# ScalarE evicts V and applies the later first normalizations; V's bias goes through the output weights

## The chip, the cores and the metric

One core of one Trainium2 chip runs the kernel. The metric is device time in microseconds (us) of one execution. Engines are named as in the profile: PE is TensorE, DVE is VectorE, ACT is ScalarE, POOL is GpSimd, SP is SyncE, which issues every DMA. A measurement of this kind tells a difference of about one per cent from none.

## What is computed

16 sequences of 128 tokens with 512 features pass through three residual blocks in 32-bit floats:

```python
x = x + attn(layernorm(x))      # 16 heads of 32, ALiBi bias, 30*tanh(s/30), causal softmax, Wo, bo
x = x + xattn(layernorm(x))     # 128 context tokens per sequence, masked softmax, readout
x = x + ffn(layernorm(x))       # gate/up/down with weights rounded to fp8 e4m3, width 1536
```

In the first block `v = h @ Wv.T + bv` and `out = (probs @ v) @ Wo.T + bo`, and each row of `probs` sums to one.

## The kernel before

The sequences are worked on in G = 4 groups of GT = 4 (512 tokens). For each group g four stages hg = 0 to 3 run, one for each four heads. One stage on PE is: `scores(g, hg)` into PSUM banks 2 to 5 (S_BANK, one for each head); the Q and K projections of the next stage into banks 0 and 1 (Q_BANK, K_BANK); other work of this stage; then `context(g, hg)`, which multiplies probabilities by V into bank 6 (C_BANK) and their sums into bank 7 (E_BANK). The other work is, at hg 0, the four V projections `v_proj` into banks 6, 7, 0, 1; at hg 1, the output projection `wo_proj` of the group before, into the same four banks; at hg 2, `turn_x`, the transposes of the next group's normalized input. Every full-precision product is made of three products of rounded halves (hi x hi, hi x lo, lo x hi), so that one projection of 128 columns is 12 matmuls of 128x512. The order on each engine is written out by hand, and each engine works strictly in it; semaphores tie them together. `take(item, b)` gives a bank to a new item once the item before it is drained, and `wait_drained` and `wait_filled` are its other two ends.

ACT, in each stage, takes tanh out of the four score banks, evicts Q with its bias (`q_out`), applies the exponential to four tiles, evicts K (`k_out`), rounds the context (`context_high`), and at hg 2 rounds the transposed input (`x_high`). POOL applies the causal mask to the four tiles (`causal`, L638), makes the low half of the context (`low_part`, L632), the reciprocal roots (`norm_scale`, L627), adds the output bias to the residual (`add_bo`, L659). DVE evicts V with its bias (`v_out`, L994), normalizes the context (`normalize_context`: reciprocal L1008, four shuffles, product L1017, after which C_BANK is free), makes the low half of the input (`x_low`, L988), adds the output projection to the residual (`wo_out`), takes statistics (`norm_stats`), and normalizes (`norm_apply`, L982).

The second block of group g - 2 lies in hg 3 and in hg 0 of later groups, in seven steps `cross(g, k)`: transpose, scores, softmax, transpose (bank 5), and the readout product into bank 3 (RO_BANK), which DVE adds to the residual with a weight (L1032, L1034, L1038).

Beside it, 36 slabs of feed-forward weights are rounded. DVE prepares a slab (`prepare_slabs`, L1058 and L1060; slab n waits until slab n - 2 is rounded), POOL rounds it (`round_slabs`, L645 and L647), ACT looks for overflows (`flag_slabs`, L811 and L813), and SP stores it and loads the sixth slab after it, once its place is flagged. Three tables, PREPARED, ROUNDED and FLAGGED, say for each group how many slabs fall in each of its four stages. After the last stage PE goes on to the feed-forward products (L262, L398), which run back to back to the end.

```python
if n > 1:
    dve.wait_ge(q_rounded, n - 1)
dve.tensor_scalar(m.bitcast(U32), w.bitcast(U32), EXPONENT_BITS, None, ALU.bitwise_and)
```

## Time and profile before

| what | us |
|---|---|
| median of three runs | 579.44 |
| lowest and highest of them | 578.35, 582.94 |
| the profiled execution | 580.64 |
| its span, first to last instruction | 578.9 |
| PE busy in the span | 551.5 |
| DVE, POOL, ACT busy | 339.7, 279.8, 243.2 |

The profile is of one execution, 1.74 us longer than its span. A timeline row gives the start in us from the span's start, the length, the engine, the line of the code, and in square brackets how long the engine stood idle before it and what released it. Rows merge instructions of one form. Ends of matmuls are modelled: the next one starts a little before the end that a row gives. The granted clock is a share of TensorE's full 2.4 GHz.

### The profile page before, as it was taken

The page shows a single profiled execution, that of the slowest core. Times are in us where ns is not written, and L with a number is a line of the kernel's source. Part 1 is how long each engine was busy: PE and PEld are TensorE (multiplying, and loading weights), DVE is VectorE, ACT ScalarE, POOL GpSimd, SP SyncE. Part 2 cuts the span into 40 slices and gives each one's busy share as a digit, 9 for nine tenths or more (in the row PEclk, how much of TensorE's full clock was granted, in tenths as well). Part 3 has the DMA queues.
Part 4 walks back from the last instruction along what each step waited for, and adds up shares of the span by engine and source line. Part 5 has one row for each costly group of instructions (what it writes and reads, how often), then busy time and mean ns, then how long its engine had stood idle before and what let it go on. Part 6 is the DMA issues. An engine that isn't in the chain of part 4 may idle for free.

```text
span 578.9 us, 9934 instructions
## 1 busy us (share of the span) xinstructions
PE 551.5 (95%) x3890; PEld 452.1 (78%) x3890; DVE 339.7 (59%) x674; ACT 243.2 (42%) x471; POOL 279.8 (48%) x284
## 2 busy tenths in 40 slices
PE   2998998999989999899999999999999999999997
PEld 2787876888768887687887787888888888888885
DVE  6478737975488754986767674345533564233322
ACT  3537882668626676237753242023311333023310
POOL 5756769855667666888767230023400343013310
PEclk9999999999999999899999999999999999999999
DMA  8861223441215420194181902100001000100001
GB/s 263 301 200 43 71 75 108 129 165 41 88 57 145 148 66 27 55 308 135 56 307 41 303 0 92 54 19 1 1 31 43 1 0 1 44 30 0 2 18 54
DMA packets 44189, 50.98 MB, mean 88 GB/s; under 512 B 3184, under 2 KB 25712, under 8 KB 44144
## 3 DMA queue, kind: packets, MB, share of 16 engines
q1 hardware_dynamic: 44144, 50.36, 26.9%
q8 instruction: 31, 0.51, 0.4%
q14 instruction: 14, 0.11, 0.1%
HBM read 36.72 MB, written 13.63 MB: 87 GB/s over the span
## 4 chain that ended last, share of the span: by engine, by line
PE 80%; POOL 7%; DVE 6%; ACT 4%; issue 1%; DMA 1%; SPq 0%; DVEq 0%; ACTq 0%
PE bank L262 52%; PE bank L398 15%; PE bank L257 3%; PE bank L336 2%; PE bank L318 2%; PE bank L354 2%; PE bank L343 2%; POOL probs L638 2%; DVE q_m L1058 1%; DVE q_m L1060 1%; POOL x_res L659 1%; PE bank L310 1%; POOL rstd L627 1%; POOL q_w L647 1%; POOL q_w L645 1%
## 5 line engine op out<-in xcount | busy, mean ns | idle before, releaser
L262 PE MATMUL bank<-reduced 128*128 128x512 f32 x1536 | 363.0, 395 | 1.6 <-DVE reduced L988 1.6
L262 PEld LDWEIGHTS bank<-reduced 128*128 128x128 f32 x1536 | 287.6, 189 | 64.4 <-issue 3.3
L742 POOL TENSOR_TENSOR f_parts<-fused,f_parts 128x512 fp32r<-128x512 f32 x48 | 62.2, 1295 | 174.8 <-ACT f_parts L929 174.8
L911 ACT ACTIVATE tanh_g<-bank,half_gate 128x512 f32<-128x512 f32 x48 | 33.1, 689 | 152.5 <-PE bank L262 152.3
L398 PE MATMUL bank<-reduced,f_parts 128*128 128x512 f32 x384 | 89.0, 391 | 0.0
L398 PEld LDWEIGHTS bank<-reduced,f_parts 128*128 128x128 f32 x384 | 71.8, 188 | 15.6 <-issue 0.8
L638 POOL TENSOR_SCALAR_AFFINE_SELECT probs<-probs 128x512 f32<-128x512 f32 x64 | 41.6, 681 | 61.8 <-ACT probs L794 61.8
L1174 DVE SCALAR_TENSOR_TENSOR silu<-tanh_g,bank 128x512 f32<-128x512 f32 x48 | 32.9, 686 | 57.4 <-ACT tanh_g L911 57.4
L789 ACT ACTIVATE probs<-bank 128x512 f32<-128x512 f32 x64 | 33.0, 602 | 50.1 <-PE bank L318 47.4
L645 POOL TENSOR_TENSOR q_w<-q_w,q_m 128x512 f32<-128x512 f32 x36 | 46.9, 1302 | 4.2 <-DVE q_m L1060 4.2
L647 POOL TENSOR_TENSOR q_w<-q_w,q_m 128x512 f32<-128x512 f32 x36 | 47.2, 1312 | 2.8
L1181 DVE SCALAR_TENSOR_TENSOR fused<-bank,fuse_c,silu 128x512 f32<-128x512 f32 x48 | 36.0, 751 | 17.6 <-PE bank L262 16.9
L1192 DVE TENSOR_TENSOR y_sb<-bank,down_c 128x512 f32<-128x512 f32 x16 | 11.1, 692 | 55.8 <-PE bank L398 55.8
L257 PE MATMUL bank<-identity,xn 128*128 128x128 f32 x192 | 26.8, 285 | 10.8 <-DVE xn L982 9.6
L794 ACT ACTIVATE probs<-probs 128x512 f32<-128x512 f32 x64 | 35.8, 625 | 0.0
L1058 DVE TENSOR_SCALAR q_m<-q_w 128x512 uint32<-128x512 uint32 x36 | 29.6, 822 | 7.7 <-POOL q_w L647 7.6
L1060 DVE TENSOR_SCALAR q_m<-q_m 128x512 f32<-128x512 f32 x36 | 33.0, 918 | 1.2
L929 ACT ACTIVATE f_parts<-fused 128x512 fp32r<-128x512 f32 x48 | 29.9, 623 | 8.6 <-DVE fused L1181 8.5
L971 DVE BATCH_NORM_STATS2 bn<-x_res 128x6 f32<-128x512 f32 x48 | 31.7, 685 | 2.8 <-DMA x_res<-in_x 2.2
L257 PEld LDWEIGHTS bank<-identity,xn 128*128 128x128 f32 x192 | 23.4, 148 | 12.5 <-issue 9.9
L811 ACT ACTIVATE q_j<-q_w 128x512 f32<-128x512 f32 x36 | 22.4, 622 | 24.2 <-POOL q_w L647 16.0
L336 PE MATMUL bank<-probs,sums_to 128*32 128x128 f32 x512 | 27.1, 283 | 5.2 <-POOL probs L638 3.0
(86 smaller groups left out, 536.2 us busy)
## 6 DMA issues: line engine op xcount, KB each, us to landing
quantized<-q_w SPq DMA_DIRECT2D x36, 256.0 KB, 3.3
reduced<-quantized SPq DMA_DIRECT2D x12, 512.0 KB, 7.5
memT_sb<-in_memT SPq DMA_DIRECT2D x16, 256.0 KB, 4.7
mem_sb<-in_mem SPq DMA_DIRECT2D x16, 256.0 KB, 5.5
out<-y_sb SPq DMA_DIRECT2D x16, 256.0 KB, 2.0
x_res<-in_x SPq DMA_DIRECT2D x3, 1024.0 KB, 7.0
q_w<-in_gate_w SPq DMA_DIRECT2D x12, 256.0 KB, 3.2
q_w<-in_up_w SPq DMA_DIRECT2D x12, 256.0 KB, 3.3
```

The costliest lines, as they stand in the source:

```text
L257: ins = pe.transpose(dst[:, k * S:(k + 1) * S], src[:, k * P:(k + 1) * P], identity[:])
L262: ins = pe.matmul(dst, stationary, moving, start=(n == 0), stop=(n == len(pairs) - 1))
L336: ins = pe.matmul(sums[rows, 0:S], sums_to[:, i, :], probs[:, j, i, :], start=(i == 0), stop=(i == GT - 1))
L398: ins = pe.matmul(dst[:], part[:, f, t], down_q[:, f], start=(f + n == 0), stop=(f + n == FT))
L638: pool.affine_select(out=probs[:, j], in_=probs[:, j], compare_op=ALU.is_ge, fill=0.0, base=0, pattern=[[0, GT], [1, S]], channel_multipli ...
L645: pool.tensor_tensor(w, w, m, ALU.add).then_inc(q_sum, 1)
L647: pool.tensor_tensor(w, w, m, ALU.subtract).then_inc(q_rounded, 1)
L742: pool.tensor_tensor(f_lo[:, f, :], fused[:, f % 2, :], f_hi[:, f, :].bitcast(F32), ALU.subtract).then_inc(f_lo_ready, 1)
L794: act.activation(probs[:, j], probs[:, j], ACT.Exp, scale=CAP).then_inc(exped, 1)
L1058: dve.tensor_scalar(m.bitcast(U32), w.bitcast(U32), EXPONENT_BITS, None, ALU.bitwise_and).then_inc(q_step, 1)
L1060: dve.tensor_scalar(m, m, MIN_NORMAL, ROUNDER, ALU.max, ALU.mult).then_inc(q_prepared, 1)
L1181: dve.scalar_tensor_tensor(fused[:, f % 2, :], ups[:], fuse_c[:, f:f + 1], silu2[:, f % 2, :], ALU.mult, ALU.mult).then_inc(drain_sem(("U" ...
```

## The change

- V is evicted by ACT without its bias (`v_out` moves from DVE to ACT, after `context_high` in stage 0, with the overflow look of slabs between).
- The bias of V is carried through the output weights instead: `bias_through` puts 12 matmuls of 128x512 between the second and third V projection of group 0, with the bias broadcast as stationary operand, into bank 5 (PT_BANK). DVE adds the result to `bo_b` (`bias_out`), and POOL's `add_bo` of group 0 waits for that and comes after the causal mask. The bias is loaded as 128x4 instead of broadcast as 128x512.
- Three later normalizations, those of groups 2 and 3 for their first block and that of group 0 for its feed-forward block (`norm_apply(g + 1)` for g = 1, 2, 3), are applied by ACT, with a shift that DVE makes (`norm_shift`, two instructions on 128x4). Group 1's stays on DVE.
- On ACT the four exponentials stand directly behind the four tanh in stages 1, 2 and 3, and `q_out` after them; at stage 2 `k_out` comes before `q_out` and `context_high` after both. Stage 0 keeps its order.
- The last readout of a group takes Q_BANK instead of RO_BANK, and the transposes at stage 2 take K_BANK before Q_BANK.
- In group 0 statistics of group 1 come before the slabs, POOL rounds no slab ahead of the causal mask in stages 2 and 3, and the three tables are changed.

The diff, without declarations and unchanged neighbours:

```diff
-ROUNDED = ((2, 1, 2, 1),) + ((4, 3, 0, 2),) * (G - 1)
-FLAGGED = ((0, 2, 1, 2),) + ((3, 4, 0, 2),) * (G - 1)
-PREPARED = ((3, 1, 2, 1),) + ((4, 3, 0, 2),) * (G - 1)
+ROUNDED = ((0, 2, 1, 2), (4, 4, 0, 2)) + ((4, 3, 0, 2),) * (G - 2)
+FLAGGED = ((0, 0, 1, 1), (4, 5, 0, 2)) + ((3, 5, 0, 2),) * (G - 2)
+PREPARED = ((2, 1, 1, 2), (4, 4, 0, 2)) + ((4, 3, 0, 2),) * (G - 2)
...
-            def cross(g, k):
+            def cross(g, k, readout=RO_BANK):
...
                     i = k - 3
-                    dst, done = take(("RO", g, i), RO_BANK)
+                    dst, done = take(("RO", g, i), readout)
...
+            def bias_through():
...
+                pe.wait_ge(bv_split, 2)
+                pe.wait_ge(w_lo_made, WO_PART + 1)
+                dst, done = take(("BO",), PT_BANK)
+                products(dst[:], [(part[:, k:k + 1].to_broadcast([P, P]), w[:, k]) for k in range(KT)
+                                  for part, w in ((bv_hi, wo_hi), (bv_hi, wo_lo), (bv_lo, wo_hi))]).then_inc(done, 1)
...
                     v_proj(g, i, (C_BANK, E_BANK, Q_BANK, K_BANK)[i])
+                    if g == 0 and i == 1:
+                        bias_through()
                     if g >= 2 and i != 2:
-                        cross(g - 2, (4, 5, None, 6)[i])
...
+                        cross(g - 2, (4, 5, None, 6)[i], RO_BANK if i < 3 else Q_BANK)
...
                 for i in range(GT):
-                    turn_x(g + 1, i, (S_BANK, S_BANK + 1, Q_BANK, K_BANK)[i])
+                    turn_x(g + 1, i, (S_BANK, S_BANK + 1, K_BANK, Q_BANK)[i])
...
             weights(V_PART)
-            for dst, src in ((bv_b[:], bv.partition_broadcast(P)), (bo_b[:], bo.partition_broadcast(P)),
+            for dst, src in ((bv_c[:], bv), (bo_b[:], bo.partition_broadcast(P)),
...
                 pool.wait_ge(xn_ready[0], (g + 1) * GT)
+                if g == 0:
+                    wait_drained(pool, ("BO",))
...
                 slabs = slabs_at(ROUNDED, g, 0)
-                if g == 0:
-                    for i in range(GT):
-                        add_bo(g, i)
-                else:
+                if g:
...
                 else:
+                    for i in range(GT):
+                        add_bo(g, i)
...
                 slabs = slabs_at(ROUNDED, g, 2)
-                round_slabs(slabs[:1])
+                if g:
+                    round_slabs(slabs[:1])
...
                 low_part(g, 1)
-                round_slabs(slabs[1:])
+                round_slabs(slabs[1:] if g else slabs)
...
                 slabs = slabs_at(ROUNDED, g, 3)
-                round_slabs(slabs[:1])
+                if g:
+                    round_slabs(slabs[:1])
...
                 low_part(g, 2)
-                round_slabs(slabs[1:])
+                round_slabs(slabs[1:] if g else slabs)
...
             ffn_low(0, 1)
-            flag_slabs(flagged[:1])
...
                 ffn_low(0, f)
-                flag_slabs(flagged[f - 1:f])
                 round_slabs(late[f - 1:f])
+                flag_slabs(flagged[f - 2:f - 1])
...
+            def v_out(g, i):
+                src = wait_filled(act, ("V", g, i))
+                act.activation(v[:, i, :], src[:], ACT.Copy).then_inc(drain_sem(("V", g, i)), 1)
...
+            def norm_apply(g):
+                act.wait_ge(shift_made, g - 1)
+                for i in range(GT):
+                    act.activation(xn1[:, i, :], token_tile(g % G, i), ACT.Identity, bias=shift[:, i:i + 1],
+                                   scale=rstd[0][:, i:i + 1]).then_inc(xn_ready[0], 1)
...
                     context_high(g - 1, 3)
-                for k in range(4, 7):
-                    flag_slabs(flagged[k - 4:k - 3])
-                    if g >= 2:
-                        cross(g - 2, k)
+                for i in range(GT):
+                    if i < 3:
+                        v_out(g, i)
+                        if g >= 2 and i < 2:
+                            cross(g - 2, 4 + i)
+                        flag_slabs(flagged[i:i + 1 if i < 2 else None])
+                    else:
+                        v_out(g, i)
...
                     tanh(g, 1, j)
-                q_out(g, 2)
...
                     exp(g, 1, j)
+                q_out(g, 2)
...
                     context_high(g, 0)
+                else:
+                    norm_apply(g + 1)
...
                     tanh(g, 2, j)
-                context_high(g, 1)
-                q_out(g, 3)
...
                 k_out(g, 3)
+                q_out(g, 3)
+                context_high(g, 1)
...
                         tanh(g, 3, j)
+                    for j in range(4):
+                        exp(g, 3, j)
                     q_out(g + 1, 0)
-                    exp(g, 3, 0)
-                    exp(g, 3, 1)
...
                         cross(g - 1, 0)
-                    exp(g, 3, 2)
-                    exp(g, 3, 3)
...
-            def v_out(g, i):
-                src = wait_filled(dve, ("V", g, i))
-                dve.tensor_tensor(v[:, i, :], src[:], bv_b[:], ALU.add).then_inc(drain_sem(("V", g, i)), 1)
+            def bias_out():
+                src = wait_filled(dve, ("BO",))
+                dve.tensor_tensor(bo_b[:], src[:], bo_b[:], ALU.add).then_inc(drain_sem(("BO",)), 1)
...
+            def norm_shift(g):
...
+                dve.wait_ge(rstd_ready[0], g + 1)
+                dve.tensor_scalar(shift[:], mv[0][:, :, 0], -1.0, None, ALU.mult).then_inc(shift_step, 1)
+                dve.wait_ge(shift_step, g - 1)
+                dve.tensor_tensor(shift[:], shift[:], rstd[0][:], ALU.mult).then_inc(shift_made, 1)
...
             dve.tensor_tensor(fuse_c[:], gate_c[:], up_c[:], ALU.mult).then_inc(fuse_c_made, 1)
+            dve.tensor_copy(bv_hi[:], bv_c[:]).then_inc(bv_split, 1)
+            dve.wait_ge(bv_split, 1)
+            dve.tensor_tensor(bv_lo[:], bv_c[:], bv_hi[:].bitcast(F32), ALU.subtract).then_inc(bv_split, 1)
...
                     prepare_slabs(slabs[1:2])
-                    v_out(g, 0)
                     cross(g - 2, 4)
-                    v_out(g, 1)
...
                     cross(g - 2, 5)
-                    v_out(g, 2)
                     prepare_slabs(slabs[3:])
-                    v_out(g, 3)
...
                 else:
-                    for i in range(GT):
-                        v_out(g, i)
-                        prepare_slabs(slabs[i:i + 1])
+                    if g == 0:
+                        next_stats(1)
+                        bias_out()
+                    prepare_slabs(slabs)
...
                     masks(g - 1)
-                else:
-                    next_stats(1)
...
                 slabs = slabs_at(PREPARED, g, 1)
-                norm_apply(0, g + 1, (g + 1) % G)
+                if g == 0:
+                    norm_apply(0, 1, 1)
+                else:
+                    norm_shift(g + 1)
...
         "bq": per_partition(a["L0_attn_bq"]), "bk": per_partition(a["L0_attn_bk"]),
-        "bv": a["L0_attn_bv"], "bo": a["L0_attn_bo"], "slopes": a["L0_attn_alibi_slopes"].reshape(HG, 4).T,
+        "bv": per_partition(a["L0_attn_bv"]), "bo": a["L0_attn_bo"], "slopes": a["L0_attn_alibi_slopes"].reshape(HG, 4).T,
```

The order on three engines, at the places where PE's waits hang on it. First VectorE, from the normalized context (0, 2) on to the one of (0, 3), which frees C_BANK for the first V projection of group 1; the pair on `q_m` is one slab's preparation. Before:

```order
L1008 RECIPROCAL rec<-bank 128x128
L1014 STREAM_SHUFFLE ctxT<-rec 128x128 x4
L1017 TENSOR_TENSOR ctxT<-bank,ctxT 128x512
L1058 TENSOR_SCALAR q_m<-q_w 128x512
L1060 TENSOR_SCALAR q_m<-q_m 128x512
L971 BN_STATS bn<-x_res 128x6 x4
L976 BN_AGGR mv<-bn 128x2 x4
L1008 RECIPROCAL rec<-bank 128x128
L1014 STREAM_SHUFFLE ctxT<-rec 128x128 x4
L1017 TENSOR_TENSOR ctxT<-bank,ctxT 128x512
L994 TENSOR_TENSOR v<-bank,bv_b 128x512
```

And now:

```order
L1047 RECIPROCAL rec<-bank 128x128
L1053 STREAM_SHUFFLE ctxT<-rec 128x128 x4
L1056 TENSOR_TENSOR ctxT<-bank,ctxT 128x512
L1097 TENSOR_SCALAR q_m<-q_w 128x512
L1099 TENSOR_SCALAR q_m<-q_m 128x512
L1003 BN_STATS bn<-x_res 128x6 x4
L1008 BN_AGGR mv<-bn 128x2 x4
L1097 TENSOR_SCALAR q_m<-q_w 128x512
L1099 TENSOR_SCALAR q_m<-q_m 128x512
L1047 RECIPROCAL rec<-bank 128x128
L1053 STREAM_SHUFFLE ctxT<-rec 128x128 x4
L1056 TENSOR_TENSOR ctxT<-bank,ctxT 128x512
```

A second preparation stands ahead of the reciprocal, and the eviction of V behind it is gone. Next GpSimd, from the causal mask of stage 3 in group 0 to that of stage 0 in group 1 (`probs` is the mask, `reduced` the context's low half, a pair on `q_w` one slab). Before:

```order
L638 AFFINE_SELECT probs<-probs 128x512 x4
L632 TENSOR_TENSOR reduced<-ctxT,reduced 128x512
L645 TENSOR_TENSOR q_w<-q_w,q_m 128x512
L647 TENSOR_TENSOR q_w<-q_w,q_m 128x512
L638 AFFINE_SELECT probs<-probs 128x512 x4
```

The one slab there is group 1's first. Now, for the same stretch:

```order
L654 AFFINE_SELECT probs<-probs 128x512 x4
L648 TENSOR_TENSOR reduced<-ctxT,reduced 128x512
L661 TENSOR_TENSOR q_w<-q_w,q_m 128x512
L663 TENSOR_TENSOR q_w<-q_w,q_m 128x512
L661 TENSOR_TENSOR q_w<-q_w,q_m 128x512
L663 TENSOR_TENSOR q_w<-q_w,q_m 128x512
L661 TENSOR_TENSOR q_w<-q_w,q_m 128x512
L663 TENSOR_TENSOR q_w<-q_w,q_m 128x512
L654 AFFINE_SELECT probs<-probs 128x512 x4
```

Three slabs stand between the two masks where one stood. Last ScalarE in stage 2 of group 1 (`probs<-bank` is tanh, `probs<-probs` the exponential). Before:

```order
L789 ACTIVATE probs<-bank 128x512 x4
L801 ACTIVATE reduced<-ctxT 128x512
L785 ACTIVATE qT<-bank,bq_c 128x512
L794 ACTIVATE probs<-probs 128x512 x4
L781 ACTIVATE kT<-bank,bk_c 128x512
L776 ACTIVATE reduced<-bank 128x4x128 x4
```

And now:

```order
L817 ACTIVATE probs<-bank 128x512 x4
L822 ACTIVATE probs<-probs 128x512 x4
L799 ACTIVATE kT<-bank,bk_c 128x512
L803 ACTIVATE qT<-bank,bq_c 128x512
L829 ACTIVATE reduced<-ctxT 128x512
L794 ACTIVATE reduced<-bank 128x4x128 x4
```

The exponentials moved ahead of Q's eviction, and Q's eviction and the context's rounding moved behind K's.

## Rows read from the trace of the kernel before

**Rows 1.** The page's first part, TensorE: busy us, share of the span, instructions.

```profile
PE 551.5 (95%) x3890; PEld 452.1 (78%) x3890; DVE 339.7 (59%) x674; ACT 243.2 (42%) x471; POOL 279.8 (48%) x284
```

**Rows 2.** Waits of TensorE: us in total, times, longest.

```profile
PE bank L257 <- DVE xn L982: 9.6, 2, 9.3
...
PE bank L354 <- DVE x_res L1038: 4.3, 2, 2.1
...
PE bank L336 <- POOL probs L638: 3.0, 2, 1.8
...
PE bank L257 <- ACT kT L781: 1.2, 1, 1.2
```

**Rows 3.** Timeline of TensorE, groups 0 and 1: start, length, instruction [idle before <-releaser].

```profile
52.74 0.43 PE L336 MATMUL bank<-probs,sums_to 128*32 128x128 f32 x8 [1.82 <-POOL probs L638]
...
55.95 5.74 PE L262 MATMUL bank<-reduced 128*128 128x512 f32 x24
...
61.53 1.91 PE L257 MATMUL bank<-identity,xn 128*128 128x128 f32 x16
...
73.52 0.43 PE L336 MATMUL bank<-probs,sums_to 128*32 128x128 f32 x8 [1.15 <-POOL probs L638]
...
76.73 16.61 PE L262 MATMUL bank<-reduced 128*128 128x512 f32 x72
...
96.98 0.43 PE L336 MATMUL bank<-probs,sums_to 128*32 128x128 f32 x8 [2.19 <-DVE v L994]
...
98.89 16.67 PE L262 MATMUL bank<-reduced 128*128 128x512 f32 x72
```

**Rows 4.** Timeline of ScalarE, groups 0 and 2.

```profile
48.24 0.69 ACT L785 ACTIVATE qT<-bank,bq_c 128x512 f32<-128x512 f32 x1 [0.89 <-PE bank L262]
...
73.00 0.62 ACT L801 ACTIVATE reduced<-ctxT 128x512 fp32r<-128x512 f32 x1
...
190.65 2.07 ACT L789 ACTIVATE probs<-bank 128x512 f32<-128x512 f32 x4 [2.57 <-PE bank L318]
```

**Rows 5.** Timeline of GpSimd, group 0, its last stage.

```profile
73.70 1.28 POOL L632 TENSOR_TENSOR reduced<-ctxT,reduced 128x512 fp32r<-128x512 f32 x1 [0.33 <-ACT reduced L801]
74.94 1.28 POOL L645 TENSOR_TENSOR q_w<-q_w,q_m 128x512 f32<-128x512 f32 x1
76.30 1.29 POOL L647 TENSOR_TENSOR q_w<-q_w,q_m 128x512 f32<-128x512 f32 x1
```

**Rows 6.** Timeline of VectorE, group 1, context 0 normalized.

```profile
101.07 0.94 DVE L1008 RECIPROCAL rec<-bank 128x128 f32<-128x128 f32 x1
...
103.01 0.69 DVE L1017 TENSOR_TENSOR ctxT<-bank,ctxT 128x512 f32<-128x512 f32 x1
```

**Rows 7.** Timeline of TensorE, groups 2 and 3, readout and projections.

```profile
165.87 1.13 PE L354 MATMUL bank<-mem_sb,x_pT 128*128 128x512 f32 x2 [2.13 <-DVE x_res L1038]
...
170.79 16.62 PE L262 MATMUL bank<-reduced 128*128 128x512 f32 x72
...
243.60 16.61 PE L262 MATMUL bank<-reduced 128*128 128x512 f32 x72
```

**Rows 8.** Timeline of VectorE, groups 2 and 3, around the last readouts.

```profile
160.81 1.43 DVE L1058 TENSOR_SCALAR q_m<-q_w 128x512 uint32<-128x512 uint32 x1 [2.80 <-POOL q_w L647]
...
163.78 1.25 DVE L1034 TENSOR_TENSOR x_w<-x_rec,valid 128x1 f32<-128x1 f32 x1
...
165.73 0.68 DVE L994 TENSOR_TENSOR v<-bank,bv_b 128x512 f32<-128x512 f32 x1
...
166.32 0.42 DVE L1058 TENSOR_SCALAR q_m<-q_w 128x512 uint32<-128x512 uint32 x1
...
240.72 0.44 DVE L1034 TENSOR_TENSOR x_w<-x_rec,valid 128x1 f32<-128x1 f32 x1
...
241.19 0.75 DVE L1038 SCALAR_TENSOR_TENSOR x_res<-bank,x_w,x_res 128x512 f32<-128x512 f32 x1
```

**Rows 9.** Window 239 to 242: us, busy of each engine, granted clock, DMA.

```profile
239.00:242.00 3.00, 3.00 (x64) 2.62 (x56) 2.93 (x6) 0.00 (x0) 3.00 (x3) 0.53 0.25 93
```

More of the change, by code:

```diff
@@ L92, in build @@
         minus_half = sb("minus_half", [P, GT], F32)
+        shift = sb("shift", [P, GT], F32)
+        bv_c = sb("bv_c", [P, KT], F32)
+        bv_hi = sb("bv_hi", [P, KT], F32R)
+        bv_lo = sb("bv_lo", [P, KT], F32R)
         gate_c = sb("gate_c", [P, FT], F32)
@@ L144, in build @@
             bias_r = sb("bias_r", [P, HG, S], F32R, att)
-            bv_b = sb("bv_b", [P, D], F32, att)
             bo_b = sb("bo_b", [P, D], F32, att)
@@ L191, in build @@
         bo_added = sem("bo_added")
+        shift_step, shift_made, bv_split = sem("shift_step"), sem("shift_made"), sem("bv_split")
         memT_loaded = [sem(f"memT_loaded{n}") for n in range(GT)]
```

## The prediction

> **What bounds the kernel now.** I read the page's first part, then TensorE's waits, then its timeline, and last the timelines of the engines that release it. PE is busy for 551.5 of 578.9 us [rows 1], so what can be won is its idle time of 27.4 us. The list of waits [rows 2] names 22.9 us of this, and the reader is to see how little of it the change can touch. The largest, 9.6 us until the first normalized input, is the start. What is left in reach are six waits of one to two us: two on the causal mask (3.0), one on V's eviction (2.19, in [rows 3]), two on a readout's addition (4.3), one on Q/K evictions (1.2). The feed-forward part has none, so a lead that PE has when it leaves the attention part is kept to the end. I therefore follow PE stage by stage and keep one number: how late (+) or early (-) it is against before.
>
> A wait costs some 0.2 more than its row says, since ends of matmuls are modelled: 55.95 + 5.74 = 61.69, but the next begins at 61.53 [rows 3]. I add 0.16 to 0.2 to each.
>
> **Group 0.** *Twelve products.* 72 products take 16.61 us [rows 3], 0.23 each; twelve add 2.8. Nothing hides them, as PE waits for nothing at V in group 0. The eviction of the last V, now ready at once, gives some 0.2 back: +2.6.
>
> *Exponentials behind tanh.* Before, ACT stood for 0.89 us until Q was filled and then evicted it (0.59 from start to next start) before the first exponential [rows 4]. Both go, and the mask chain is 1.5 us sooner, while PE comes 2.6 later. So PE's wait of 1.82 before context (0, 1) is gone: +2.6 - 2.0 = +0.6. The same at context (0, 3): 1.15 + 0.2 goes.
>
> *A new delay at x_low.* Slab 2 is prepared only when POOL has rounded slab 0, which now comes after the context's low part. By the links of the next paragraph this is 53.3 (K filled, 52.74 + 0.6) + 1.33 + 1.24 + 2.65 = 58.5, and DVE has normalized context (0, 1) at 58.5 + 2.8 + 2.6 = 63.9. `context_high`, `x_high` and `x_low` follow it, and Q for group 1 needs all four low halves. I estimate 0.6 (0 to 0.9) from these lengths: +1.2, and after context (0, 3) -0.1.
>
> *A new wait at the first V of group 1.* This is the largest term against the change. V (1, 0) needs C_BANK, which is free when DVE has normalized context (0, 3), and slab 5's preparation now stands ahead of that and waits for slab 3. Counted from the point where PE has finished K (1, 0), before at 73.52 - 1.15 = 72.37 [rows 3]: POOL's low part begins 1.33 later, at 73.70 [rows 5], since K's eviction and the context's rounding (at 73.00, [rows 4]) lie between; the slab 1.24 after that; it takes 77.59 - 74.94 = 2.65 [rows 5]. Then the preparation beside POOL's next slab, 2.8 (two times 1.4, as at 160.81 in [rows 8]), then from the reciprocal to the product's end 103.70 - 101.07 = 2.63 [rows 6]. Sum 10.65, with 0.05 for a semaphore 10.7. PE reaches V (1, 0) at 76.73 + 24 x 0.231 = 82.27, which is 8.75 after context (0, 3) began at 73.52 [rows 3], and the change lets that context begin at once. Wait 10.7 - 8.75 = 1.95 (1.2 to 2.6): +1.9.
>
> **Group 1.** V (1, 3) is evicted by ACT. Before it stands the overflow look of two slabs, 2 x 1.3, begun after V (1, 2); it ends as V (1, 3) fills, so the wait of 2.19 goes with 0.2: -0.5. Then `wo_proj` needs C_BANK. Before, it was free at 103.70 [rows 6] and wanted at 98.89 + 5.55 = 104.44 [rows 3], a reserve of 0.74. PE now comes 2.35 sooner against DVE's chain, which is paced by POOL's slabs and gains only V's 0.68 [rows 8] and some contention: a wait of 0.5 (0 to 1.4). Late by 0 when group 2 begins.
>
> *Normalizations on ACT.* Four instructions of about 0.6, and one more slab's look of 1.3, add 3.7 us to stage 1 of groups 1 to 3. They lie in idle time: ACT stood 2.57 us before tanh (2, 2) [rows 4] and 2.7 and 2.3 before that. PE turns the result only at stage 2. Cost 0; were the cover gone, each us beyond 7.5 would cost one per group. The reorder at stage 2 makes `x_high` start 1.7 us after K fills instead of 0.6, and it ends 0.1 before PE wants it: 0 (to 0.2 per group).
>
> **Groups 2 and 3.** The readout that waited 2.13 [rows 7] takes Q_BANK, and so goes at once; but Q_BANK is then wanted by Q (2, 2) after context and scores. PE would be there at 170.79 - 2.13 - 0.4 (refill, twice) - 0.6 (an issue gap before the scores) = 167.7. DVE drains it after: readout 2 ends at 165.73; one slab's preparation 0.8 to 1.4; weight 0.35; product 0.75, so 168.0 to 168.5 [rows 8]. Start 168.3: gain 2.5.
>
> In group 3 the same count gives less. Before, Q (3, 2) began at 243.60 [rows 7]. DVE's small product for the weight lay beside POOL's flag additions, started at 240.72, and ended with them at 241.16; the readout was added by 241.94 [rows 8]. Without two evictions of V DVE is there 1.2 sooner but meets the same POOL instruction, so that it ends at the same time: Q (3, 2) starts at 242.0. Gain 1.6, though PE would be there some 4 us sooner. In 239 to 242 PE ran with a granted clock of 0.53, the lower of its two levels (1.2 of 2.4 GHz), after it had stood for 2.14 us [rows 9]; about 1.6 us were lost there, and this is the 1.6 that comes back.
>
> The Trainium skill bears on this place (SBUF — State Buffer, Who interferes with whom): VectorE's second port pair is GpSimd's too, an exclusive lock, which a VectorE instruction with one SBUF input outside the 2-port modes does not need. By it V's eviction, with one input from PSUM, never held GpSimd up, so that its removal gives back its own 0.6 alone, which speaks against the move. The trace agrees in that `v_out` takes 0.68 everywhere, while the weight's product of 128x1 takes 0.44 to 1.25 beside GpSimd. Without such a lock group 3 would gain 2.6.
>
> *Last wait.* The 1.2 us on K's eviction in group 3 [rows 2] came from `context_high` standing ahead of Q's and K's evictions and waiting for DVE. It stands behind them now. A fifth slab's look delays tanh (3, 2) by 1.3, which the shorter path covers: gain 1.2.
>
> **Sum.** +2.6 - 2.0 + 0.6 - 1.3 + 2.0 - 2.4 + 0.5 = 0 for groups 0 and 1; -2.5 - 1.6 - 1.2 = -5.3 for groups 2 and 3. Against the profiled execution, 580.64, this is 575.3; its span is 578.9, and the 1.7 around it do not change. The median of the runs is 579.44, so I predict 579.4 - 5.3 = 574.1.
>
> **The rivals.**
> *The waits simply go.* If DVE stays ahead of PE in groups 0 and 1 (`x_low`, C_BANK twice: 0.6 + 2.0 + 0.5 = 3.1) and the readout's bank is free in time, gain is 5.3 + 3.1 + up to 0.8: 570.2 to 571. For it: the 8.75 and 10.7 above differ by only 1.95, and DVE is busy for 59%. Against: the code makes slab 5 wait for slab 3, and each link of that chain has its row.
> *The weight's product does not wait for POOL in group 3.* Then DVE drains the bank 1.0 sooner: 573.1.
> *A new wait brings the clock down.* PE stands two us before V (1, 0), as long as before the stretch at 0.53 [rows 9]; three such waits in the trace (2.19, 2.13, 2.14) gave one fall. Price 1.6, and with C_BANK's wait at its upper bound 1.4 in place of 0.5: 574.1 + 1.6 + 0.9 = 576.6.
> *Slower than before: the readout in Q_BANK.* It puts DVE's last readout ahead of Q (g, 2) in groups 2 and 3. If each of its preparation's two instructions and its weight's product meets a POOL instruction of 1.3, the bank is drained at 165.73 + 1.4 x 3 + 0.75 = 170.7, and with one more such delay 172.1, so that group 2 loses 1.3 instead of winning 2.5, group 3 likewise 1.3 instead of 1.6: -5.3 + 3.8 + 2.9 = +1.4, 580.9. It decides from a draining after 170.8. Against: in the row POOL was idle then, and the preparation took 0.42 at 166.32 [rows 8].
>
> **Chances.** Forecast 0.50, waits simply go 0.25, no wait for POOL 0.08, clock 0.12, slower 0.05. The range is 570.5 to 577.8: it takes in most of the second case and all of the fourth. A measurement tells about 1% (5.8 us) from no change; 573.6 is that bound. Faster by more: most of the second case, the third, and a sixth of the first, 0.41. Slower by more: 0.02. Between: 0.57.
>
> **What would show it.** Right: PE waits of about two us before its first V of group 1, released by the context's normalization; under one us before the first output projection; the first context of groups 2 and 3 without waits, and Q behind the scores waiting for a readout's addition; no masks in the list of waits; twelve products of 0.23 in group 0; ACT idle ahead of tanh (2, 2). Wrong: no wait at V (1, 0), a wait of PE on V or on a normalized input made by ACT, or another stretch of the lower clock.

## The result, and the profile after

The changed kernel takes 576.96 us (median of 20 runs, 574.90 to 580.39), the one before 580.78 (20 runs, 578.27 to 583.67). The ratio is 0.9936, 95% interval 0.9917 to 0.9955: a little faster, by less than the one per cent that a measurement of this kind tells from none. Forecast were 574.1 and a range of 570.5 to 577.8. The profiled execution has a span of 575.3 us, before 578.9.

The page's first part after the change, to be laid beside [rows 1]:

```profile
PE 552.0 (96%) x3902; PEld 452.2 (79%) x3902; DVE 325.3 (57%) x655; ACT 260.3 (45%) x499; POOL 280.1 (49%) x284
```

ACT has taken 17 us of work over and DVE has lost 14. PE has twelve matmuls more. TensorE's waits after the change (us in total, times, longest), beside [rows 2]:

```profile
PE bank L261 <- DVE xn L1014: 9.2, 2, 8.9
PE bank L266 <- DVE x_res L1077: 3.9, 2, 2.3
PE bank L266 <- DVE ctxT L1056: 3.1, 2, 2.0
```

Behind the start of scores (0, 0) no mask, no V and no eviction of K is waited for any more; two waits for a bank that DVE normalizes out of (`ctxT`) are new, and the two on a readout's addition (`x_res`) are nearly as long as before, only in another place: ahead of Q and no longer ahead of the next readout. TensorE's timeline, columns as in [rows 3]:

```profile
37.63 5.60 PE L266 MATMUL bank<-reduced 128*128 128x512 f32 x24
...
60.88 2.17 PE L261 MATMUL bank<-identity,xn 128*128 128x128 f32 x16
...
83.41 11.14 PE L266 MATMUL bank<-reduced 128*128 128x512 f32 x48 [1.99 <-DVE ctxT L1056]
...
104.57 11.14 PE L266 MATMUL bank<-reduced 128*128 128x512 f32 x48 [1.14 <-DVE ctxT L1056]
...
169.76 16.61 PE L266 MATMUL bank<-reduced 128*128 128x512 f32 x72 [1.58 <-DVE x_res L1077]
...
241.19 16.58 PE L266 MATMUL bank<-reduced 128*128 128x512 f32 x72 [2.33 <-DVE x_res L1077]
```

The first row is the third V projection of group 0, behind the twelve products, which begin at 34.86 and so take 2.77. The next to last row is what became of the 2.13 in [rows 7]. VectorE ahead of the wait at 83.41:

```profile
77.85 1.43 DVE L1097 TENSOR_SCALAR q_m<-q_w 128x512 uint32<-128x512 uint32 x1 [5.29 <-POOL q_w L663]
79.31 1.40 DVE L1099 TENSOR_SCALAR q_m<-q_m 128x512 f32<-128x512 f32 x1
80.63 0.94 DVE L1047 RECIPROCAL rec<-bank 128x128 f32<-128x128 f32 x1
...
82.57 0.69 DVE L1056 TENSOR_TENSOR ctxT<-bank,ctxT 128x512 f32<-128x512 f32 x1
```

DVE stands 5.29 us for a slab on POOL with the context that PE waits for queued behind it. VectorE ahead of the wait at 169.76:

```profile
166.08 0.93 DVE L1097 TENSOR_SCALAR q_m<-q_w 128x512 uint32<-128x512 uint32 x1
167.04 0.43 DVE L1099 TENSOR_SCALAR q_m<-q_m 128x512 f32<-128x512 f32 x1
167.39 0.16 DVE L1071 RECIPROCAL x_rec<-x_den 128x1 f32<-128x1 f32 x1
167.58 1.25 DVE L1073 TENSOR_TENSOR x_w<-x_rec,valid 128x1 f32<-128x1 f32 x1
168.87 0.75 DVE L1077 SCALAR_TENSOR_TENSOR x_res<-bank,x_w,x_res 128x512 f32<-128x512 f32 x1
```

The product of 128 numbers (L1073) takes 1.25 us and ends with the POOL instruction beside it, which that same preparation had released:

```profile
167.55 1.26 POOL L661 TENSOR_TENSOR q_w<-q_w,q_m 128x512 f32<-128x512 f32 x1 [0.83 <-DVE q_m L1099]
```

The same place before, on VectorE, with V's eviction between the preparation and the product:

```profile
166.78 0.43 DVE L1060 TENSOR_SCALAR q_m<-q_m 128x512 f32<-128x512 f32 x1
167.12 0.68 DVE L994 TENSOR_TENSOR v<-bank,bv_b 128x512 f32<-128x512 f32 x1
167.72 0.15 DVE L1032 RECIPROCAL x_rec<-x_den 128x1 f32<-128x1 f32 x1
167.91 0.68 DVE L1034 TENSOR_TENSOR x_w<-x_rec,valid 128x1 f32<-128x1 f32 x1
168.62 0.75 DVE L1038 SCALAR_TENSOR_TENSOR x_res<-bank,x_w,x_res 128x512 f32<-128x512 f32 x1
```

POOL's instruction ran from 167.28 for 1.28 there, and the product, begun later, took 0.68 to the same end. From the end of the preparation to the end of the readout's addition it is 2.16 us before and 2.15 now: what the missing eviction freed, the product spends beside POOL.

**How traces of different kernels are compared here.** Two things differ between profiles where the code is the same. The first 24 Q/K products take 5.7 us in some and 7.3 to 8.6 in others, and the granted clock falls to half for some 3.4 us in some (both in the last section). So I give each profile a number of its own, in the last column: its span, less the start of scores (0, 0) on PE, less 1.64 for each such fall (where e8's 72 products took 18.22 in place of 16.58). For e1's first fall, a long one, 2.7 is taken (13.82 in place of 11.14). The price is an upper one: in e4 and at e1's second fall the same 72 products took 17.92 and 17.95, a loss of 1.34, so that 0.3 too much may be taken off for a fall. Each ratio is to runs of the kernel before that stood beside that kernel; the medians of those were 580.8 to 582.8, so that the ratios can be compared across rows, and the medians only roughly.

| kernel | median, us (runs) | ratio to before, 95% | scores (0, 0) at | falls | span from there, at full clock |
|---|---|---|---|---|---|
| before | 580.78 (20) | 1 | 24.08 | 1 | 553.2 |
| changed | 576.96 (20) | 0.9936 [0.9917, 0.9955] | 22.74 | 0 | 552.6 |
| e1 | 581.00 (10) | 0.9986 [0.9958, 1.0014] | 23.30 | 2 | 552.2 |
| e4 | 576.65 (10) | 0.9926 [0.9902, 0.9950] | 23.11 | 1 | 551.6 |
| e5 | 574.34 (4) | 0.9879 [0.9834, 0.9924] | 23.73 | 0 | 549.3 |
| e6 | 572.07 (4) | 0.9843 [0.9793, 0.9893] | 21.75 | 0 | 548.7 |
| e2 | 580.07 (10) | 0.9989 [0.9964, 1.0013] | 21.65 | 0 | 555.2 |
| e3 | 575.14 (4) | 0.9909 [0.9875, 0.9942] | 21.50 | 0 | 549.8 |
| e7 | 584.17 (8) | 1.0072 [1.0034, 1.0110] | 21.68 | 2 | 556.3 |
| e10 | 577.60 (5) | 0.9948 [0.9931, 0.9966] | 21.11 | 1 | 553.2 |
| e8 | 577.50 (7) | 0.9919 [0.9894, 0.9944] | 20.45 | 1 | 552.6 |
| e9 | 589.81 (4) | 1.0131 [1.0093, 1.0168] | 21.64 | 2 | 560.9 |
| e11 | 570.46 (6) | 0.9810 [0.9780, 0.9841] | 21.51 | 0 | 547.3 |
| e12 | 583.63 (10) | 1.0043 [1.0017, 1.0069] | 23.31 | 2 | 556.9 |

### The profile page after: what moved, and what is told of

The parts are those of the page before. It is cut to its first block, busy times and chain, and to the rows that moved or that the text cites. A ratio compares the mean times of both kernels' runs of the same rounds, so it can differ in the third digit from the quotient of the medians.

```text
span 575.3 us, 9972 instructions
## 1 busy us (share of the span) xinstructions
PE 552.0 (96%) x3902; PEld 452.2 (79%) x3902; DVE 325.3 (57%) x655; ACT 260.3 (45%) x499; POOL 280.1 (49%) x284
## 4 chain that ended last, share of the span: by engine, by line
PE 82%; POOL 6%; DVE 6%; ACT 3%; issue 1%; DMA 1%; SPq 0%; DVEq 0%
PE bank L266 55%; PE bank L402 15%; PE bank L261 4%; PE bank L340 2%; PE bank L322 2%; PE bank L347 2%; PE bank L358 1%; DVE q_m L1099 1%; DVE q_m L1097 1%; POOL x_res L677 1%; POOL q_w L663 1%; POOL q_w L661 1%; POOL probs L654 1%; POOL rstd L643 1%; POOL reduced L648 1%
## 5 line engine op out<-in xcount | busy, mean ns | idle before, releaser
L1097 DVE TENSOR_SCALAR q_m<-q_w 128x512 uint32<-128x512 uint32 x36 | 25.3, 704 | 34.6 <-POOL q_w L663 33.0
L648 POOL TENSOR_TENSOR reduced<-ctxT,reduced 128x512 fp32r<-128x512 f32 x16 | 20.7, 1295 | 23.5 <-ACT reduced L829 23.5
```

## The experiments

### e1: the context of stage 0 ahead of the last slab

```diff
-PREPARED = ((2, 1, 1, 2), (4, 4, 0, 2)) + ...
+PREPARED = ((2, 1, 1, 1), (5, 4, 0, 2)) + ...
```

> The changed kernel with slab 5 prepared after the normalization of context (0, 3) instead of ahead of it (PREPARED one slab later). Theory: the wait of 1.99 us before V (1, 0) is this preparation's alone; it goes, VectorE normalizes the context at once, and the time falls by 2.0 less what comes back at the next wait for C_BANK (1.1 in the changed kernel, paced by GpSimd's slabs, which move only with slab 5): between 1.0 and 2.0 us below the changed kernel's 577. Rival: the bank is late for another reason (the context's sums, GpSimd's low part), then a wait of over 1 us stays at V (1, 0).

The wait of 1.99 at the first V of group 1 is gone, so its cause is the slab ahead of the context, as the prediction has it. But TensorE then waits longer at the next use of C_BANK, and the clock falls:

```profile
104.96 13.82 PE L266 MATMUL bank<-reduced 128*128 128x512 f32 x48 [3.27 <-DVE ctxT L1056]
```

```profile
104.00:108.00 4.00, 3.04 (x7) 0.50 0.00 0
```

(The second fence is the stretch from 104 to 108 us: its length, PE busy, matmuls, granted clock, DMA share and GB/s.) 1.99 + 1.14 of the changed kernel have become 3.27 in one piece: DVE normalizes context (1, 0) at the same distance from the start, 81.5 against 81.7 (104.82 - 23.30 and 104.42 - 22.74). A wait was moved, none was removed, and the expected gain of 1.0 to 2.0 did not come. At full clock e1 would be level with the changed kernel (552.2 and 552.6, with 0.3 of doubt); all ten of its runs had a mean granted clock of 0.996 or less, which made it a loss.

### e4: the masks of the second block behind the context

```diff
+                normalize_context(g, 0)
                 if g:
                     masks(g - 1)
-
-                normalize_context(g, 0)
```

> The changed kernel with the attention mask's three VectorE instructions behind the context's normalization of stage 0 instead of ahead of it. Theory: C_BANK comes free 2.3 to 2.9 us sooner in group 1, the wait of 1.14 us before the first output projection goes, and nothing else moves: 1.1 to 1.4 us below the changed kernel. Rival: VectorE is late as a whole, so that the wait moves to the two output projections' additions in the same stage and the time stays.

The 1.14 before the output projection is gone, a wait of 0.74 on a score tile of ACT appears some 14 us later, 1.99 stays. It wins 1.0 in the last column, 0.7 if its fall is priced at its own 1.34, against the 1.1 to 1.4 expected, and nothing that the median shows.

### e5: the last readout's addition ahead of the slab

```diff
                     cross(g - 2, 5)
-                    prepare_slabs(slabs[3:])
                     cross(g - 2, 6)
+                    prepare_slabs(slabs[3:])
```

> The changed kernel with the last readout's addition ahead of the last slab preparation of stage 0 in groups 2 and 3. Theory: the waits of 1.58 and 2.33 us before Q (2, 2) and Q (3, 2) are the preparation's and the weight's small product, both beside GpSimd; without the preparation ahead they shrink by its 1.3 and 2.3 us, to 0.3 and near 0: 2.5 to 3.9 us below the changed kernel. Rival: the small product waits for GpSimd wherever it stands, then each wait shrinks by under 1 us.

Both waits on `x_res` are gone from TensorE's list; 3.3 us of 3.9 are won. On VectorE, in group 2:

```profile
165.15 1.26 DVE L1073 TENSOR_TENSOR x_w<-x_rec,valid 128x1 f32<-128x1 f32 x1
...
167.30 0.47 DVE L1073 TENSOR_TENSOR x_w<-x_rec,valid 128x1 f32<-128x1 f32 x1
167.80 0.75 DVE L1077 SCALAR_TENSOR_TENSOR x_res<-bank,x_w,x_res 128x512 f32<-128x512 f32 x1
```

The first lies beside POOL's slab (165.12 to 166.39). The second begins beside the other half of it (166.47 to 167.75) and ends with it at 167.77, so it pays 0.47 only since it began late. What PE waited for was the place behind the slab.

### e6: the three together

> The three edits together (slab 5 after the normalization, masks after the normalization, readout ahead of the preparation). Theory: the four waits of 1.99, 1.14, 1.58 and 2.33 us are each local, the gains add up to 5 to 7 us below the changed kernel, near 571. Rival: GpSimd's slabs pace the stages, so that what is won at one place is waited for at the next, and the sum is under 3 us.

The last column falls by 3.9, between what the theory (5 to 7) and the rival (under 3) gave: the four waits came to 7.0 us, and a part of that is waited for elsewhere. PREPARED as in e1 loses nothing here, since the masks no longer stand behind it; of the two `ctxT` waits 0.42 is left. The largest wait is a new one, in group 1, before Q of the next stage:

```profile
117.13 5.73 PE L266 MATMUL bank<-reduced 128*128 128x512 f32 x24 [2.23 <-DVE x_res L1040]
```

with VectorE, which adds the third tile of the output projection (L1040), ahead of it:

```profile
110.49 1.43 DVE L1097 TENSOR_SCALAR q_m<-q_w 128x512 uint32<-128x512 uint32 x1 [1.31 <-POOL q_w L663]
...
116.31 0.68 DVE L1040 TENSOR_TENSOR x_res<-bank,x_res 128x512 f32<-128x512 f32 x1
```

### e2: the last readout back in RO_BANK

```diff
-                        cross(g - 2, (4, 5, None, 6)[i], RO_BANK if i < 3 else Q_BANK)
+                        cross(g - 2, (4, 5, None, 6)[i])
```

> The changed kernel with the last readout back in its old bank (RO_BANK instead of Q_BANK). Theory: the readout waits again for the addition of the one before it, by 2.1 us in groups 2 and 3, and Q behind the scores waits no more; the swap was worth only the difference of the two waits (before 2.13 and 2.14, after 1.58 and 2.33 us plus refill), so this kernel is 0.5 to 1.5 us slower than the changed one. Rival: the swap is what won the time, then it is 3 to 4 us slower.

Waits of 2.13 and 2.12 stand again before the readout, as in [rows 7], and gaps of up to 1.21 in which PE waits for nothing shown lie before the scores. 2.6 us are lost, between the theory's 0.5 to 1.5 and the rival's 3 to 4: that much the other bank is worth.

### e3: without the twelve products

```diff
                     v_proj(g, i, (C_BANK, E_BANK, Q_BANK, K_BANK)[i])
-                    if g == 0 and i == 1:
-                        bias_through()
```

`bias_out` and POOL's wait for it go too; V's bias is left out of the result.

> The changed kernel without the twelve products, their addition to the output bias and GpSimd's wait for it: V's bias is left out. Theory: twelve products of 0.23 us lie bare on TensorE, but without them TensorE comes sooner to the masks of stage 1 and 3 in group 0, and waits there: of 2.8 us some 2.0 to 2.8 come back. Rival: they fill time in which TensorE would wait for the masks anyway (before: 1.82 and 1.15 us), then under 1 us comes back.

2.8 us less in the last column, the 2.77 of the products' own time. The other waits are the changed kernel's (1.99, 1.18, 1.63, 2.35) and no mask is waited for, so nothing hides the products, as argued.

### e7: V evicted by DVE again

`v_out` moves back to VectorE's places of before, as an addition of zeros, while the bias stays in the products.

> The changed kernel with V evicted by VectorE again, in the old places (adding zeros from a tile instead of the bias, so with the same operands as before). Theory: the wait on V (1, 3) comes back, 2.2 us and 0.2 for the refill, and in groups 2 and 3 the two evictions behind the fifth cross step delay Q by some 0.6 to 1.3 us each: 3 to 5 us slower than the changed kernel. Rival: with the tables changed VectorE has room, and it is under 1 us.

3.7 us slower in the last column (the medians differ by 7.2; none of its eight runs had a mean granted clock above 0.997), and TensorE's list of waits has V again:

```profile
PE bank L359 <- DVE v L1021: 5.4, 2, 2.7
PE bank L341 <- DVE v L1021: 2.8, 2, 1.9
```

8.2 on V, less what they take the place of (3.9 on `x_res` and one `ctxT` of 1.1), make 3.2 of it. Moving V to ACT is the part of the change that earns the products' 2.8. The readout's weight behind V's eviction takes 0.67 again, and from the preparation's end to the addition's end it is 2.15 once more.

### e10: only ACT's order, in the kernel before

Exponentials behind tanh, K's and Q's evictions ahead of `context_high`, K_BANK before Q_BANK.

> The kernel before with the order of exponentials and evictions of the changed one alone (and the order of its banks for the transposes). Theory: the waits on masks go (1.82 and 1.15 us with 0.2 each), so does the one of 1.2 on K's eviction in group 3: 3.5 to 4.7 us below the kernel before, though up to 1 is lost by the later rounding of the transposed input. Rival: TensorE then meets the next wait sooner (the normalized context, V), and under 2 us are won.

Mask waits go from 3.0 to 0.3 and the 1.2 on K vanishes, but V takes their place:

```profile
PE bank L336 <- DVE v L992: 4.2, 3, 2.2
```

where it was 2.19. 553.2 is 553.2: alone, the new order wins nothing behind scores (0, 0), and the expected 3.5 to 4.7 did not come from there. The runs are 0.5% faster all the same. The profile has that in its start, 21.11 against 24.08, and 2.91 of these 2.97 us are the first 24 products (5.70 against 8.61, last section). All five runs have spans of 575.3 to 576.1, where such a start with one fall gives 575.9. Whether the order has to do with it or five runs met it by chance, no run settles.

### e8: the later normalizations back on DVE

> The changed kernel with the three later normalizations back on VectorE, everything else as changed. VectorE gets four instructions of 0.5 to 1.0 in place of two of 0.5, so 1 to 3 us more ahead of the additions of the output projection. Theory (the move to ScalarE frees VectorE where it is late): in group 1 the third addition ends at 118.10 now and TensorE wants its bank at 118.9, so that TensorE waits 0.2 to 2.2 there; in groups 2 and 3 VectorE has 3.7 us of idle time in that stage and nothing is lost. Time 577.2 to 579.2 against 577.0. Rival (the prediction as it stands, cost and gain 0): no new wait of TensorE, 577.0.

The rival, which is the prediction's own term, holds: every wait is the changed kernel's, 552.6 is 552.6. This part costs and gives nothing.

### e9: ACT's old order in the changed kernel

```diff
                 for j in range(4):
                     tanh(g, 2, j)
+                context_high(g, 1)
+                q_out(g, 3)
                 for j in range(4):
                     exp(g, 2, j)
                 k_out(g, 3)
-                q_out(g, 3)
-                context_high(g, 1)
```

and likewise at stages 1 and 3, and the transposes' banks.

> The changed kernel with ScalarE's old order of evictions and exponentials. Theory (the prediction's terms): the wait for the mask at context (0, 1) returns with its 1.82 + 0.2, that at context (0, 3) with 1.15 + 0.2, which is then taken off the wait of 1.99 at the first V of group 1, and the wait on the eviction of K in group 3 with 1.2: 577.0 + 2.0 + 1.2 = 580.2, and V's wait is 0.6 to 0.8. Rival (the new order only moves time, since the normalized context sets the pace): 577.0 within 0.6.

Both expectations fail: 589.8, and 8.3 us in the last column (12.9 in the medians, with two falls in the profile). ScalarE in stage 2 of group 0, and behind it TensorE's transposes:

```profile
61.76 0.63 ACT L829 ACTIVATE reduced<-ctxT 128x512 fp32r<-128x512 f32 x1 [4.23 <-DVE ctxT L1058]
62.30 0.67 ACT L803 ACTIVATE qT<-bank,bq_c 128x512 f32<-128x512 f32 x1
62.86 2.17 ACT L822 ACTIVATE probs<-probs 128x512 f32<-128x512 f32 x4
64.94 0.67 ACT L799 ACTIVATE kT<-bank,bk_c 128x512 f32<-128x512 f32 x1
```

```profile
63.02 0.66 PE L261 MATMUL bank<-identity,xn 128*128 128x128 f32 x4 [1.04 <-ACT qT L803]
65.67 1.11 PE L261 MATMUL bank<-identity,xn 128*128 128x128 f32 x4 [1.99 <-ACT kT L799]
```

ACT stands 4.23 us for the context, with Q and K queued behind. In the kernel before, the same instruction at the same place did not wait at all: a slab stood ahead of that context on DVE there too, but POOL rounded two slabs in stage 0 (now none), so that DVE did not stand for it. 5.6 on K, 1.4 on Q, 2.3 on masks and 0.6 on a score tile, less 1.1 of `ctxT`, make 8.8.

### e12: e9 with that slab behind the context

```diff
-PREPARED = ((2, 1, 1, 2), (4, 4, 0, 2)) + ...
+PREPARED = ((2, 0, 2, 2), (4, 4, 0, 2)) + ...
```

> The kernel with ScalarE's old order, which took 589.8 us, with one number of PREPARED moved in group 0 from (2, 1, 1, 2) to (2, 0, 2, 2), so that slab 2 is prepared behind the normalization of context (0, 1) and not ahead of it. There ScalarE had stood 4.23 us for that context with Q's and K's evictions behind it, and the transposes had waited 1.04 and 1.99 for them, at half clock afterwards. Theory (ScalarE's old order and the new tables collide: an eviction that TensorE wants is queued behind a wait for a slab): both waits in group 0 go with 0.2 each, and the stretch at the lower clock, some 1.5: 589.8 - 4.9 = 584.9 (583.5 to 586), while the 1.64 in group 1 stays. Rival (the old order is slow in itself, through the waits on the masks and on K): 589 to 590.

```profile
59.05 0.65 ACT L829 ACTIVATE reduced<-ctxT 128x512 fp32r<-128x512 f32 x1
60.08 0.69 ACT L803 ACTIVATE qT<-bank,bq_c 128x512 f32<-128x512 f32 x1 [0.38 <-PE bank L266]
```

The wait is gone. From scores (0, 0) to scores (0, 3) it is 43.35 us (66.66 - 23.31) instead of 48.19 (69.83 - 21.64): 4.84, where 4.9 was worked out, the fall in that stretch of e9 included. The median falls by 6.2 to 583.63, within what was expected; by the ratios it is some 5. In the last column 4.0 of e9's 8.3 are won. The other 4.3 stay, with waits of 3.6 on K and 2.3 on masks: half of e9's loss is the collision of the old order with the new tables, and the rest is waits that the old order has in the new schedule anyway.

### e11: four orders

e6, and:

```diff
-                    prepare_slabs(slabs[2:])
                     wo_out(g - 1, 2)
+                    prepare_slabs(slabs[2:])
```

> The kernel with the three orders on VectorE, and a fourth: the third addition of the output projection stands ahead of the last slabs' preparation, not behind them. In the kernel with three orders the one long wait left is 2.23 us, of TensorE for that addition in group 1 (117.13), while VectorE stood idle for 1.31 us at 109.18, just after the third tile was full. Theory (the addition is late only because of its place): it runs in that idle stretch, the wait of 2.23 and its 0.2 go, and the time is 572.1 - 2.4 = 569.7, span about 568. Rival (the preparation of slabs is pushed back and the lateness comes out again at the next context, 128x512 to be drained from C_BANK, or at the low part of the context behind them): the wait turns up again with 1 us or more behind the stage, time 571 to 572.

The 2.23 is gone; a 0.98 appears at 125.18 (TensorE for `x_low`), so that 1.4 of the 2.4 stay. What is left of TensorE's waits behind the start:

```profile
PE bank L314 <- DVE reduced L1020: 1.0, 1, 1.0
PE bank L340 <- POOL probs L654: 0.5, 1, 0.5
PE bank L314 <- issue: 0.5, 1, 0.5
PE bank L322 <- ACT kT L799: 0.4, 1, 0.4
PE bank L266 <- DVE ctxT L1056: 0.4, 1, 0.4
```

570.46 us beats both kernels: ratio 0.9810 to before, and 5.3 us below the changed kernel in the last column. Three of the four edits only swap two neighbours on VectorE, and the fourth changes two numbers of a table.

## Why the prediction was right, and where it was off

The verdict, within one per cent, was the likeliest class, and the time lies in the range, 2.9 above the forecast. The steps were in the main the right ones, but the number owes something to luck. Of the forecast gain of 5.3, 1.6 was the clock and 3.7 the schedule; of the schedule the traces show 0.6 (553.2 to 552.6). The rest of the measured 3.8 came from the start and from rarer falls of the clock, which the forecast did not have in that way. Step by step, as lateness against before; measured is the difference of the two timelines plus 1.34, by which the changed kernel's scores (0, 0) began sooner:

| TensorE reaches | predicted | measured |
|---|---|---|
| scores (0, 1) | +2.6 | +2.5 |
| scores (0, 2) | +0.6 | +0.7 |
| Q for group 1 | +1.2 | +1.6 |
| scores (1, 0) | -0.1 | +0.3 |
| first V of group 1 | +1.9 | +2.5 |
| scores (1, 1) | -0.5 | +0.2 |
| scores (1, 2) | 0 | +1.5 |
| Q (2, 2) | -2.5 | +0.3 |
| Q (3, 2) | -4.1 | -1.1 |
| scores (3, 3) | -5.3 | -2.2 |

- **Twelve products, mask waits, the wait at the first V.** Right in place and size: 2.77 for 2.8, 1.99 for 1.95, and e1 and e3 show both causes.
- **C_BANK at the output projection, mis-sized.** I took 0.5 between 0 and 1.4; it was 1.14 and 0.2. The mask copy (L1059) took 1.51 beside POOL, where it had taken 0.41. This is the step that made scores (1, 2) late by 1.5, and e4 removes it.
- **Transposes.** At stage 2 they take 2.17 instead of 1.91 in each group; I had 0 to 0.2 for it.
- **Group 2, mis-sized.** I took the weight's product for 0.35. Its own row before has 0.68, beside POOL, and I had counted V's eviction ahead of it as time won. With the eviction gone the product begins together with POOL's slab, at 1.25, and nothing is won on VectorE there (2.15 for 2.16; e7, with V back, has 2.15 too). The gain is 1.4 (from +1.7 at scores (2, 0) to +0.3), not 2.5, and PE came to group 2 late by the 1.7 of the steps above, where I had it at 0. In group 3, where the same meeting was counted, 1.6 came for 1.6, and it is what before's fall of the clock had cost: the changed kernel's profile has none. The Trainium skill (SBUF — State Buffer, Who interferes with whom) describes an exclusive lock, by which a VectorE instruction with two inputs from SBUF, like this one, waits for a GpSimd instruction that reads SBUF. The rows agree: the same instruction takes 0.47, 0.68 or 1.25, each time to the end of POOL's.
- **Last wait.** 1.18 for 1.2.
- **Normalizations on ACT.** 0 predicted, 0 by e8.
- **The clock.** I counted before's stretch of half clock [rows 9] as a loss of 1.6 that the change brings back. It is a chance, not a fixed part. In 64 runs of the kernel before that stood beside the experiments, 17 had a mean granted clock of 0.998 or more, and their median span is 577.0; of the 20 runs of the changed kernel 14 had it, median 574.6. At equal clock the gain is thus 2.4 us, and the rest of the 3.8 is that falls are rarer, 6 of 20 against 47 of 64. Within the 2.4 the traces give the change's own stages 0.6 (553.2 to 552.6). The sooner start of the profile gives 1.3, of which 0.9 are the first 24 products (7.67 against 8.61), code that the change does not touch. The spans at full clock say the same: the 14 of the changed kernel lie in two bunches, seven at 573.2 to 574.1 and seven at 575.1 to 575.9. With the early start of e8 or e6 the profile's 552.6 would make 573.1 to 574.4, and with its own late one it makes 575.3. Of before's 17 none is below 576.4, though 553.2 with e10's early start would make 574.3. Why before never starts early is not shown.

So where did the expected gain go? 3.7 us of PE's idle time are gone (six waits with 10.7 on V, masks, K and the readouts before, four with 7.0 on `ctxT` and readouts after), and some 0.2 for each of the two waits fewer. The products take 2.8 of that back, and the three sets of transposes 0.8. That leaves 0.5, and the last column has 0.6. Of the parts, V on ACT is worth 3.7 (e7) and the readout's bank 2.6 (e2); the order on ACT is worth 8.3 within the change (e9) and nothing before it (e10), so the values do not add up: each was a cover for another. The rival that the waits simply go was wrong for the schedule as written; in e11, where nearly all of them are gone, the time is what that rival gave, 570.5 for 570.2 to 571.

## What to carry to other kernels

When a table or a row of instructions is shifted so that a slow neighbour's work (here POOL's slabs) paces an instruction that TensorE waits for, look at what stands directly ahead of each bank's release and swap the two before moving work to another engine: four such edits gave 5.3 us at full clock, and the change as a whole 0.6. No run tried them in the kernel before, where they might have given as much without the move. Price a small VectorE instruction for the place it will have after the change, not for the one it has in the trace: here it took 0.68 behind V's eviction and 1.25 without it. And undo parts one at a time in both kernels: an order worth nothing alone (e10) can be what keeps the rest from costing 8 (e9).

## What I had not expected of the hardware

**The clock falls after some waits and not after others of the same length.** The granted clock went from 1.00 to 0.50 (from 2.4 to 1.2 GHz) for 3.4 us (e1's first for 6.8), beginning between 1.1 us before and 1.5 us after TensorE took up work again. Over all fourteen profiles there are 30 waits of 1.88 us or more behind the start (two close ones of e9 counted as one): 11 were followed by such a fall, and one of eleven between 1.5 and 1.88. The same wait before Q (3, 2) shows both; e8, and then the changed kernel, with 2.35 and 2.33 us of idle time ahead:

```profile
240.00:244.00 4.00, 4.00 (x12) 0.57 0.49 152
```

```profile
242.00:246.00 4.00, 4.00 (x19) 1.00 0.52 150
```

e11, with no wait over one us behind the start, had a mean clock of 1.00 in each of its six runs, e6 0.999 or more in its four. So a wait of two us costs, beside itself, a chance of 1.3 to 1.6 us more; what decides it in a given run stays open.

**The first Q/K products run at either clock, and the window does not show it.** 24 products of 128x512 take 5.7 us in eight of the fourteen profiles and 7.27 to 8.61 in six, with the DMA engines full in both. e6, then the changed kernel:

```profile
15.17 5.71 PE L266 MATMUL bank<-reduced 128*128 128x512 f32 x24 [1.61 <-DVE reduced L1020]
```

```profile
14.20 7.67 PE L266 MATMUL bank<-reduced 128*128 128x512 f32 x24 [1.61 <-DVE reduced L1020]
```

Two windows of the changed kernel, TensorE alone:

```profile
15.00:18.00 3.00, 3.00 (x8) 1.00 1.06 358
18.50:21.50 3.00, 3.00 (x15) 1.00 1.02 382
```

Both give a granted clock of 1.00, yet the first has half as many products. They start 0.427 us apart there, as in e1's stretch at 0.50 (seven in 3.04 us), and 0.23 apart in the second. The trace's records of the clock begin only at 18.41, and the products change pace at just that time, so the 1.00 of the first window stands for no record: the lower level (1.2 GHz) is what the spacing shows. All fourteen traces have it so. In the six with slow first products the records begin at 18.4 to 20.7, in the eight others at 11.7 to 14.0, before the first product (13.9 to 15.2). TensorE had done the same before either, 16 transposes from 8.9 to 10.0 us on, and a pause of 1.6 to 1.7 behind them. What makes the clock rise early or late stays open. It is worth up to 2.9 us (8.61 against 5.70), more than the whole of this change at full clock, so a difference of a few tenths of a per cent between two kernels should be looked for there first.
